# First layer of a graph network: the mask of far nodes by an operation with a constant tensor as its second factor

## The reference, cut to what matters

```
amax = segment_max(a, dst)
ex = exp(a - amax[dst])
alpha = ex / (segment_sum(ex, dst)[dst] + 1e-16)
agg = segment_sum(alpha * h, dst)
```

## Time and profile before

| | us |
|---|---|
| median of 3 runs | 10575.95 (10566.82 to 10586.68) |
| the profiled execution | 10573.21 |
| its span, first to last instruction | 10571.2 |
| PE busy | 8497.0 (80%) |
| DVE busy | 7420.9 (70%) |
| POOL busy | 6191.2 (59%) |
| ACT busy | 3241.5 (31%) |

### The profile page before, as it was taken

How to read it: one execution, slowest core, us unless ns; L and a number is a source line. 1 busy time by engine, 2 the same in 40 slices (tenths; PEclk the granted TensorE clock), 3 DMA queues, 4 the chain that set the end, 5 groups by cost and what they waited for, 6 DMA issues and landing times. The chain is left out here.

```text
span 10571.2 us, 201187 instructions
## 1 busy us (share of the span) xinstructions
PE 8497.0 (80%) x50848; PEld 6425.6 (61%) x50849; DVE 7420.9 (70%) x18020; ACT 3241.5 (31%) x8443; POOL 6191.2 (59%) x6291
## 2 busy tenths in 40 slices
PE   1388888888888888888888888877658888888888
PEld 1277777777777777777777777766433333333335
DVE  2477777777777777777777777666237777777775
ACT  0133333333333333333333333322222222222223
POOL 0266666666666666666666666543007777677774
PEclk9599999999999999999999999888558888889889
DMA  2133333333333333333333333222002222222221
GB/s 35 48 83 81 83 83 81 82 83 82 81 85 81 84 83 81 83 83 82 83 82 82 83 81 83 71 61 52 8 12 57 57 57 58 58 57 57 57 57 48
DMA packets 560992, 725.68 MB, mean 69 GB/s; under 512 B 228019, under 2 KB 334899, under 8 KB 560956
## 3 DMA queue, kind: packets, MB, share of 16 engines
q0 software_dynamic: 225792, 385.65, 16.3%
q1 hardware_dynamic: 335164, 339.61, 12.1%
HBM read 708.76 MB, written 16.06 MB: 69 GB/s over the span
## 5 line engine op out<-in xcount | busy, mean ns | idle before, releaser
L739 PE MATMUL bank_pair<-w_msg,blocks 128*128 128x160 f32 (+1 forms) x15640 | 2420.7, 318 | 768.1 <-DVE blocks L983 768.1
L739 PEld LDWEIGHTS bank_pair<-w_msg,blocks 128*128 128x128 f32 x15640 | 2314.5, 219 | 859.3 <-DVE blocks L983 859.3
L1377 POOL DMA_INDIRECT gotf<-f_tab,idx x1568 | 1712.8, 1092 | 748.5 <-issue 383.9
L697 POOL DMA_INDIRECT got_src<-src_tab,idx x1568 | 1520.4, 970 | 726.6 <-POOL idx L691 368.3
L697 POOL DMA_INDIRECT got_dst<-dst_tab,idx x1568 | 1495.8, 954 | 529.3 <-issue 527.5
L761 PEld LDWEIGHTS bank_pair<-weights_t,product 128*128 128x128 f32 x12896 | 1493.9, 194 | 309.1 <-issue 294.9
L761 PE MATMUL bank_pair<-weights_t,product 128*128 128x128 f32 x12896 | 1570.5, 281 | 8.9 <-ACT weights_t L885 8.2
L1417 PE MATMUL bank_pair<-val,to_node 128*128 128x449 f32 x3136 | 1477.3, 619 | 6.0 <-DVE val L1520 6.0
L706 POOL TENSOR_TENSOR edge<-rbf,y 128x512 f32<-128x512 f32 x391 | 661.1, 1691 | 1244.5 <-PE bank_pair L728 1137.5
L894 ACT ACTIVATE weights<-near,small 128x512 f32<-128x512 f32 x391 | 282.2, 722 | 3014.1 <-DVE small L933 3014.1
L1468 ACT ACTIVATE val<-pre,y_edge 128x160 f32<-128x160 f32 x1568 | 542.9, 417 | 1894.1 <-DVE pre L1508 1894.1
(11 more groups left out here) (267 smaller groups left out, 12953.8 us busy)
## 6 DMA issues: line engine op xcount, KB each, us to landing
rbf<-in_rbf SPq DMA_DIRECT2D x392, 256.0 KB
dst_bc<-in_dst_rows SPq DMA_DIRECT2D x391, 256.0 KB
y<-in_y SPq DMA_DIRECT2D x392, 128.0 KB
y<-in_y SPq DMA_DIRECT2D x392, 96.0 KB
got_src<-src_tab,idx POOLq DMA_INDIRECT x1568
got_dst<-dst_tab,idx POOLq DMA_INDIRECT x1568
gotf<-f_tab,idx POOLq DMA_INDIRECT x1568
rbf<-in_rbf SPq DMA_DIRECT2D x392, 32.0 KB
```

The costliest lines, as they stand in the source:

```text
L697: pool.indirect_dma_start(out=buf[slot][:, t, :], out_offset=None, in_=table[:, :], in_offset=bass.IndirectOffsetOnAxis(ap=idx[slot][:, c: ...
L739: return nc.tensor.matmul(to, blocks[rows, k, P * t:P * t + P], w_msg[rows, c0:c1], start=start, stop=stop)
L1377: pool.indirect_dma_start(out=got[k % 2][:, t, :], out_offset=None, in_=f_tab[:, :], in_offset=bass.IndirectOffsetOnAxis(ap=idx[k % 2][:, ...
```

## The change

A tile `all_least` of 128x512 f32 is filled once with -1e30 before the first layer's loop. The mask of the regular step is then made by an operation that compares `dst_bc` with the partition's scalar `ring` as before, and multiplies the outcome by `all_least`, element by element, instead of by the constant -1e30. Inputs, output, order and semaphores stay.

```diff
+        all_least = tmp("all_least", [P, GE])
...
                     dve.memset(sums[:, 100:BLOCKS, :], 0.0)
+                    dve.memset(all_least[:], LEAST)
...
-                        dve.tensor_scalar(far[:], dst_bc[other][:], ring[:, at_group(g - 1)], LEAST, ALU.not_equal,
-                                          ALU.mult).then_inc(s["far"], 1)
+                        dve.scalar_tensor_tensor(far[:], dst_bc[other][:], ring[:, at_group(g - 1)], all_least[:], ALU.not_equal,
+                                                 ALU.mult).then_inc(s["far"], 1)
```

## The result

The changed kernel takes 10781.16 us (median of 4 runs, 10775.38 to 10788.41) against 10575.04 us beside it (4 runs, 10566.82 to 10586.68): ratio 1.0194, 95% interval 1.0177 to 1.0212. That is +206 us where +34 were forecast, and also above the +106 that the mask's own delay comes to.

What follows compares the result with a forecast made beforehand. The prediction took alternating DVE and TensorE work in the first layer as the bound: 391 x 0.27 = 106 us, two thirds given back by TensorE's clock, leaving 35, with the memset +36. Forecast 10610 us, range 10570 to 10690.

Steps and rivals of the forecast that it cites:

- The ring as the bound: First layer: DVE (10.13 us) and TensorE (7.46 us) take turns in each group, with the mask `far` unhidden in DVE's part.
- The operation alone: Mask `far` (L1024), unblocked: 512 elements take 0.75 us instead of 0.48, +0.27 us.
- D, half rate: Mask: two f32-sized SBUF tensors stream at half speed, +0.80 us a group, 10886 us in all; chance 0.04.
- Held by `edge`: Mask still waits for GpSimd's `edge` and ends 0.55 us behind it instead of 0.28; duration 1.76 us.
- C: Mask: GpSimd lets the two-tensor operation pass, 0.75 us instead of 1.49, 10325 us in all; chance 0.06.
- `msg` at 1.98 us, covered: GpSimd's `msg` (L710), queued behind `edge`, goes from 1.71 to about 1.98 us; GpSimd's 2.93 us of spare time covers the delay.
- The memset: Filling the constant tile, once: 512 elements on 32 partitions take 0.48 us, +0.5 us at most.
- The sum on the ring: First layer's 391 groups at +0.27 us each: 106 us, before any answer of the clock.
- What answers: TensorE's clock: First layer: fewer groups slowed, the mean stays 17.06 us, two thirds of the added time given back, 35 us left.
- A, no give-back: TensorE's clock returns none of the mask's added time: 10679 us; chance 0.19.
- B, full give-back: Disturbed groups too end in the same mean, so the price vanishes: 10573 to 10590 us; chance 0.20.

Runs made afterwards that it cites:

- the PSUM column: The changed kernel with its second factor read from one repeated column of PSUM instead of an SBUF tile: 10118.43 us against 10575.02 for the kernel before, ratio 0.9570.
- the unused tensor: The kernel before with the tile `all_least` allocated and filled but not used: 12516.41 us against 12526.69 for the kernel before, ratio 0.9993.
- the first chip: The chip of the first follow-up runs, where the unaltered kernel before took 12526.69 us, and 12532.58 us in a second set.

## Why the prediction was wrong, point by point

- **The ring as the bound: right.** Whatever was put into it or taken out, +0.11 to -0.75 us, showed in the time on the chips of this kind, and TensorE's idle time ahead of the messages grew by 101.7 us, 391 x 0.26. On the two chips with some 12520 us it is the bound in a part of the groups at most.
- **The operation alone, 0.75 us: right** (737 ns at the shortest), in part by luck. The 0.06 us of start-up that led from 0.68 to 0.75 don't come out of the numbers beside them: both start-ups are 0.22 us at that slope. D, half rate, would have been 1.28 us, and falls. What was cited beside D isn't borne out: 512 elements with two SBUF sources, one int32 and one f32, took 737 ns.
- **Held by `edge`, ending 0.55 us behind it: right** (1260.75 against 1260.20; median 1762 ns for a forecast of 1.76 us). C falls, and the PSUM column shows its condition: the operation passes with one SBUF input, not with two. The row that spoke for C, L1006 starting 0.04 us behind `edge`, didn't carry over to an operation that starts 0.5 us behind.
- **`msg` at 1.98 us, covered: right** (1979 ns); GpSimd still waits for TensorE 938.7 us in 300 waits from 1000 to 6900 us. **The memset:** 0.48 us, and the unused tensor alone 0.9993, measured only on the first chip.
- **The sum on the ring, 106 us: right** (101.7).
- **"What answers: TensorE's clock": this step failed, and in its sign.** The term had the clock give back 70 us (two thirds of 106); the runs showed it taking another 84 to 100, with the message matmuls busy 151 us longer. Two things were wrong in it. Groups were taken to come in two kinds only, so that a mean of 17.06 us could be kept by mixing them. But there are longer groups too, as the one of 18.97 us with twice the time at 0.50, and the longer ring makes them common: between 1000 and 6000 us 20 groups took over 18.5 us before, and 57 after. And a balance seen at one length of the ring was carried to another without a row that shows it. Nothing stayed at 17.06: from 1000 to 6000 us there are now 282 groups, 17.73 us each, where there were 291, 17.18 each.
- **A, no give-back, 10679,** was the nearest case and right that the balance doesn't hold, but 102 us short. The sentence "a longer idle time could bring the clock down more often" was there, at no price. Its price was to be had from the earlier trace rows: groups disturbed by a longer hold took 18.1 us instead of 17.06, 1.0 us more each. Were all 391 groups such, it would be some 400 us; as an end of the range it would have held the result. **B, full give-back,** falls with the same step.

What stays open: why the cost rises up to a ring of 0.3 to 0.4 us more and then falls (the runs show the curve, not the rule behind it); whether up to some 50 us of the change's 206 are the new operation's own; and what makes two of the five chips of the experiments run the same kernel in some 12520 instead of 10570 us. That the groups of some 19 us come about *because* the idle gap meets the previous slow stretch was argued from single groups, and not tried by itself.

## What to carry to other kernels

Where TensorE and another engine take turns, a change of one link's length is priced twice: the link times the number of rounds, which can be worked out to a few per cent, and the clock's answer, which can't be read off one balance and was here between +100 and -91 us for links 0.1 to 0.5 us longer (the +100 with the new operation in it; +55 was the most with idle work alone). Pad the link with idle work of several lengths and measure, before an operation in it is changed. And for a VectorE operation that stands still behind GpSimd's product, neither the quick form with one tensor nor a form with two SBUF tensors is the way out: what passed was a form with its second factor in PSUM, 0.27 us slower alone and 0.75 us quicker in place, or the quick form at a place in the order where GpSimd isn't in its product: 4.3% either way, and nothing or a loss of 1.1% on the first chip.

## What the runs showed of the hardware that was not expected

- The cost of a longer ring isn't monotone: with the old mask +53, +132, +188, +93 us for +0.11, +0.20, +0.36, +0.47 us, and with the new one +190 to +206 and +143 us for +0.27 and +0.46.
- VectorE's operation with an int32 tensor and a broadcast column of PSUM runs 741 ns beside GpSimd's running product, and with the constant in SBUF 1762 ns.
- The same kernel has two times by chip, 10559 to 10575 us in four of the sets of runs and 12517 to 12533 in three. On the second kind TensorE's weight loads wait 504 times in 5000 us for nothing that the profile shows instead of 290, which comes to a third of the difference at most; a change worth 4.3% on the one kind is worth nothing or costs 1.1% on the other. The kernel before must run beside every experiment.
